# A graph network's softmax over edges: the restart penalties of the running maximum move from ScalarE to GpSimd

## What is computed

```
msg     = relu(h[src] + e) + 1e-7            e = edge_attr @ We + be
m       = msg * t
seg_max = segment_max(m, dst)
ex      = exp(m - seg_max[dst])
agg     = segment_sum(msg * ex, dst) / segment_sum(ex, dst)
z       = relu(layernorm((h + agg) @ w1 + b1)) @ w2 + b2
```

## Time and profile before

| | |
|---|---|
| median of 3 runs | 3566.0 us (3565.28 to 3567.18) |
| profiled execution, span from first to last instruction | 4412.7 us |
| mean granted TensorE clock in it | 0.771 |
| POOL busy | 2517.9 us (57%), 2621 instructions |
| PE busy | 2914.6 us (66%) |
| DVE busy | 2824.3 us (64%) |
| ACT busy | 1741.2 us (39%) |

### The profile page before, as it was taken

One profiled execution on the slowest core, in us unless ns is written; L12 is line 12 of the kernel. 1 busy time (PEld: TensorE's weight loads), 2 busy tenths in 40 slices (PEclk: granted clock), 3 DMA queues, 4 the chain that ended last, 5 costly groups with the idle time before them and its releaser, 6 DMA issues.

```text
span 4412.7 us, 44760 instructions
## 1 busy us (share of the span) xinstructions
PE 2914.6 (66%) x16648; PEld 1382.9 (31%) x16648; DVE 2824.3 (64%) x2795; ACT 1741.2 (39%) x2192; POOL 2517.9 (57%) x2621
## 2 busy tenths in 40 slices
PE   3667677775437776777435777777742777777764
PEld 2223233332313333333222333333331333333333
DVE  6467678778436665666753666665763565666675
ACT  3356555545223333333432333333432333433343
POOL 6565656564366665666445666665627565655642
PEclk6778788877568888888656888887855787888875
DMA  6677778877237777777534777777734677777761
GB/s 153 162 219 204 215 195 222 219 198 174 59 100 204 204 204 192 204 204 204 133 81 115 204 204 204 205 205 201 191 76 104 160 199 199 204 202 190 211 153 40
DMA packets 1041338, 774.25 MB, mean 175 GB/s; under 512 B 914394, under 2 KB 935391, under 8 KB 1017504
## 3 DMA queue, kind: packets, MB, share of 16 engines
q1 hardware_dynamic: 934256, 446.17, 42.9%
q10 hardware_dynamic: 22048, 226.63, 14.0%
q0 software_dynamic: 84816, 98.59, 9.9%
HBM read 478.68 MB, written 292.44 MB: 175 GB/s over the span
## 4 chain that ended last, share of the span: by engine, by line
PE 41%; issue 23%; DVE 11%; ACT 10%; another core or an unknown queue 10%; POOL 4%; DMA 1%; SPq 0%; ACTq 0%; POOLq 0%; DVEq 0%
PE X L537 32%; PE X L520 5%; POOL gath L479 4%; DVE decay L885 3%; PE X L547 2%; DVE state_all L916 2%; ACT msg L647 2%; DVE X L890 1%; ACT shared L676 1%; ACT X L649 1%; ACT decay L659 1%; ACT X L664 1%; DVE state_all L900 1%; ACT decay L637 1%
## 5 line engine op out<-in xcount | busy, mean ns | idle before, releaser
L479 POOL DMA_INDIRECT gath<-z_table,idx x2488 | 2396.0, 963 | 1606.0 <-issue 750.5
L537 PE MATMUL X<-one_hot,z_parts 128*64 128x512 fp8e5 x13800 | 2103.0, 427 | 840.8 <-issue 773.1
L537 PEld LDWEIGHTS X<-one_hot,z_parts 128*64 128x64 bf16 x13800 | 939.4, 120 | 2071.2 <-issue 1542.8
L883 DVE TENSOR_TENSOR decay<-decay,top 128x1 f32<-128x1 f32 x216 | 34.2, 158 | 1358.5 <-ACT X L649 1179.6
L647 ACT ACTIVATE msg<-X,edge_bias 128x1024 f32<-128x1024 f32 (+2 forms) x216 | 228.2, 1057 | 1622.5 <-remote 1080.3
L520 PE MATMUL X<-attr,enc_edge 128*128 128x512 f32 x824 | 469.3, 688 | 221.9 <-issue 115.8
L659 ACT ACTIVATE decay<-X 128x1024 f32<-128x1024 f32 (+2 forms) x216 | 209.3, 969 | 791.7 <-DVE X L890 556.1
L871 DVE STREAM_TRANSPOSE rows_all<-state_all 128x1024 f32<-128x1024 f32 (+3 forms) x432 | 505.9, 1171 | 7.5
L885 DVE TENSOR_TENSOR_SCAN decay<-X,decay 128x1023 f32<-128x1023 f32 (+2 forms) x216 | 477.2, 2209 | 7.7
L900 DVE TENSOR_TENSOR_SCAN state_all<-decay,state_all,X 128x1024 f32<-128x1024 f32 (+2 forms) x216 | 468.2, 2167 | 20.0 <-ACT X L664 16.0
L916 DVE TENSOR_TENSOR_SCAN state_all<-decay,state_all,X 128x1024 f32<-128x1024 f32 (+2 forms) x216 | 468.0, 2167 | 0.0
(11 more groups left out here) (155 smaller groups left out, 1182.3 us busy)
## 6 DMA issues: line engine op xcount, KB each, us to landing
rows_table<-rows_all SPq DMA_DIRECT2D x784, 256.0 KB
one_hot<-one_hot_dram ACTq DMA_DIRECT2D x69, 1920.0 KB
attr<-attr_t SPq DMA_DIRECT2D x196, 512.0 KB
one_hot<-one_hot_dram ACTq DMA_DIRECT2D x69, 1280.0 KB
one_hot_dram<-one_hot SPq DMA_DIRECT2D x23, 1920.0 KB
gath<-z_table,idx POOLq DMA_INDIRECT x2488
one_hot_dram<-one_hot SPq DMA_DIRECT2D x23, 1280.0 KB
keep<-keep_dram SPq DMA_DIRECT2D x192, 128.0 KB
```

Of the source, the lines that this page charges most:

```text
L479: pool.indirect_dma_start(out=gath[s][:, n * F:(n + 1) * F], out_offset=None, in_=z_table, in_offset=bass.IndirectOffsetOnAxis(ap=idx[:, c ...
L537: last = nc.tensor.matmul(x[h * F:(h + 1) * F, BANK:CH], z_parts[:, i * GB + k, third, :], one_hot[:, i, k, h * BANK:(h + 1) * BANK], star ...
```

## The change

The function `penalties` moves from ACT's stream to POOL's, as a `tensor_scalar` with a multiply and an add. POOL makes the penalties of chunk c - 2 while it is at the gathers of chunk c: ahead of the ninth where the chunk has 16, and ahead of the first where it has fewer. The last two of a layer follow its last gathers. The waits for `keep_landed` and `num_ready` move along.

```diff
--- before.py
+++ after.py
@@ -46,6 +46,7 @@
 KEY_SLOTS = 3
 KEEP_CHUNKS = 2
 KEEP_SLOTS = 2
+LEAD = 2
 NKEEP = -(-NCH // KEEP_CHUNKS)
 GB = 5
 PIECES_1H = NT // GB
@@ -462,6 +463,17 @@
                                         in_offset=bass.IndirectOffsetOnAxis(ap=row_i[:, i:i + 1], axis=0))\
                     .then_inc(keys_gathered[i % KEY_SLOTS], 16)
 
+            def penalties(layer, c):
+                g = layer * NCH + c
+                s = g % SLOTS
+                w = width(c)
+                k, at = layer * NKEEP + c // KEEP_CHUNKS, STARTS[c] - STARTS[c - c % KEEP_CHUNKS]
+                pool.wait_ge(keep_landed[k % KEEP_SLOTS], 16 * HALVES * (k // KEEP_SLOTS + 1))
+                if g >= SLOTS:
+                    pool.wait_ge(num_ready, g - SLOTS + 1)
+                nc.gpsimd.tensor_scalar(decay[s][:, 0:w], keep8[k % KEEP_SLOTS][:, at:at + w], BIG, -BIG, ALU.mult, ALU.add)\
+                    .then_inc(pen_ready, 1)
+
             for layer in range(LAYERS):
                 if layer == 0:
                     pool.wait_ge(idx_landed, 16)
@@ -474,7 +486,10 @@
                     if g >= SLOTS:
                         pool.wait_ge(x_ready, g - SLOTS + 1)
                     settle()
+                    pause = KT if gathered_tiles(layer, c) == KT else first_tile(c) * HALVES
                     for n in range(first_tile(c) * HALVES, gathered_tiles(layer, c) * HALVES):
+                        if n == pause and c >= LEAD:
+                            penalties(layer, c - LEAD)
                         col = STARTS[c] // P * HALVES + n
                         pool.indirect_dma_start(out=gath[s][:, n * F:(n + 1) * F], out_offset=None, in_=z_table,
                                                 in_offset=bass.IndirectOffsetOnAxis(ap=idx[:, col:col + 1], axis=0))\
@@ -482,6 +497,8 @@
                     if layer == 0 and c in PREP_CHUNKS:
                         gather_keys(c - PREP_CHUNKS[0])
 
+                for c in range(NCH - LEAD, NCH):
+                    penalties(layer, c)
                 pool.wait_ge(stored[0], 16 * NSTORE * ((layer + 1) * NCH // 2 + ((layer + 1) * NCH) % 2))
                 pool.wait_ge(stored[1], 16 * NSTORE * ((layer + 1) * NCH // 2))
                 pool.wait_ge(ends_stored, 16 * (layer + 1))
@@ -626,17 +643,6 @@
 
         @block.scalar
         def _(act):
-            def penalties(layer, c):
-                g = layer * NCH + c
-                s = g % SLOTS
-                w = width(c)
-                k, at = layer * NKEEP + c // KEEP_CHUNKS, STARTS[c] - STARTS[c - c % KEEP_CHUNKS]
-                act.wait_ge(keep_landed[k % KEEP_SLOTS], 16 * HALVES * (k // KEEP_SLOTS + 1))
-                if g >= SLOTS:
-                    act.wait_ge(num_ready, g - SLOTS + 1)
-                nc.scalar.activation(decay[s][:, 0:w], keep8[k % KEEP_SLOTS][:, at:at + w], ACT.Copy,
-                                     scale=BIG, bias=-BIG).then_inc(pen_ready, 1)
-
             def messages(layer, c):
                 g = layer * NCH + c
                 s = g % SLOTS
@@ -742,10 +748,8 @@
             act.wait_ge(consts_set, 5)
             for layer in range(LAYERS):
                 for c in range(NCH):
-                    if c == 0:
-                        penalties(layer, 0)
-                        if layer == 0:
-                            act.wait_ge(t_landed, 16)
+                    if layer == 0 and c == 0:
+                        act.wait_ge(t_landed, 16)
                     messages(layer, c)
                     n = one_hot_bank(layer, c + 3)
                     building = n is not None and built_in(layer, n)
@@ -754,8 +758,6 @@
                     exponents(layer, c)
                     if building:
                         spread_lanes(n, range(2, GB))
-                    if c < NCH - 1:
-                        penalties(layer, c + 1)
                     if layer == 0 and c in PREP_CHUNKS:
                         count_keys(c - PREP_CHUNKS[0])
                     if layer > 0:
```

## The result

| | before | after |
|---|---|---|
| median | 3565.64 us (4 runs, 3564.68 to 3567.18) | 3776.74 us (4 runs, 3773.53 to 3778.55) |
| ratio, 95% interval | | 1.0591 (1.0577 to 1.0604) |
| profiled execution, span | 4412.7 us | 3773.6 us |

The change makes the kernel 211 us slower; forecast were 279. One thing must be said of the profiles: that of the kernel before shown above is of an execution like those of a second chip, on which the same kernel takes 4423 us (median of 7); the timed runs are like those of a first chip, on which it takes 3567. The span of the kernel after is within 3 us of its median.

A forecast was written before the change was run, and what follows sets the result against it. POOL's gathers were taken to bound the timed execution. 3566 us plus 252 (280 us of penalties on POOL, a tenth hidden) plus 27 at the layers' ends gave 3845 us, range 3555 to 3950.

The forecast's parts named there:

- The bound: POOL's gathers bound the timed execution, 30 us for a pair of chunks, with hardly any wait for PE.
- partly hidden: POOL bounds only part of each layer, PE or transfers the rest; half is hidden: 3706 us or less, chance 0.08.
- wholly hidden: The 0.30 us between gathers are the profiler's, so POOL's slack takes in the 280 us: 3566, chance 0.09.
- faster: POOL has slack and DVE waits for ACT, so `m` comes up to 0.97 us earlier: 3514 us, chance 0.14.
- profiled execution's frame: In the longer profiled execution penalties fit into POOL's waits for PE, so its span grows less, to 4440 to 4520 us.
- The instructions: 216 penalties on POOL: 225 us for the columns at 1.09 ns each, plus 23 us fixed at 0.105 each.
- The step to the neighbours: Step between a gather and a penalty on POOL, 0 to 0.30 us: 0.15 taken, 32 us in all.
- A tenth hidden: A tenth of POOL's added 280 us is covered, in nearly tied layer 0 and the fill of the layers, leaving +252.
- The layers' ends: At each layer's end the last full chunk's penalties come later and DVE starts 6.8 us later: 4 × 6.8 = +27 us.
- The sign named for it: A longer wait of POOL ahead of L494 was to show the cost at the layers' ends; no size given.
- POOL and DVE hold each other up: Penalties beside DVE's building of banks in layer 0 wait as gathers do: 76 us more, 3921, chance 0.06.
- The moved waits: Mid-layer, later penalties hold nothing up: the way to `x_ready` takes about 20 us, POOL needs it some 40 us later.

The follow-up runs named there:

- runs 1 to 3: run 1, run 2, and the kernel before with 78 gathers left out in layers 1 to 3: 3470.7 us.
- ACT twice: The kernel before with ACT making the penalties twice, the first time into a tile that nobody reads: 3567.2 us, ratio 0.9999.
- run 1: The kernel before, unchanged, for a second profile: 3565.3 us.
- run 2: The kernel before with ACT's penalties kept and POOL making as many on tiles of its own (the copies): 3762.4 us, ratio 1.0553.

## Why the prediction was right

**The bound.** Right, and by the argument given: POOL's own stream, added up, left no room in 3566 us for the waits for PE that the profile showed. The rivals *partly hidden* and *wholly hidden* are out (runs 1 to 3), *faster* too (ACT twice: 0.9999). One reason in it was wrong: the 846.7 us between span and median are not of profiling, as run 1 has a span of 3563.3 us for a time of 3565.3. By PE's single matmuls, which only the second chip's profiles share, they are most likely of that chip. With this the sentence on the "profiled execution's frame" falls. The span was forecast at 4440 to 4520 and is 3773.6, simply the kernel's time on the chip of the timed runs. The argument held since POOL's own durations are the same in both (963 and 967 ns a gather, 0.30 a step). The waits for others that it took from that frame were 144 us too long and the end 15 us. That is where the 114 us came from by which its sum exceeded the median; of the two explanations that it gave, the shorter ends of the layers were the right one.

**The sum.** 279 forecast, 211 measured, term by term:
- The instructions: 248 us (225 + 23) forecast, 217 measured. The slope is 0.86 ns, near the memset's 0.78 and not in the middle with 1.40; the fixed part is 0.19 us, not 0.105.
- The step to the neighbours: +32 us forecast, between 0 and 65. Measured is less than nothing: 0.99 us from gather to gather for an instruction of 1.06, about -15 us in all. The bound was wrong on this side: a tensor instruction after a gather saves a part of the gather's 0.30, and "below nothing" was left out without a reason. This is the largest error, 47 us.
- A tenth hidden, -28 us: some 10 were, and not where it was put. Even the nearly tied layer 0 has no cover between its gathers: the copies of run 2 make it 52.6 us longer from first to last gather (7 of these us are the held-up copies), layer 1 49.8. What is covered lies behind the last gathers, where the ends of the four layers are 9 to 10 us shorter than in run 1.
- Together these are 252 us forecast; the rows give 217 - 15 - 10 = 192, and run 2 gave 195, with 7 us of held-up copies in layer 0.
- The layers' ends: 27 us forecast. The changed kernel is 14 us over the copies, 21 without the 7 us that those were held up, and one chunk less of lead gives 14 back. The mechanism fits: later penalties, later end. The sign named for it did not come, a longer wait ahead of the gathers of the sums: POOL waits 52.7 us for the stores there (28.5 + 24.2) and waited 99.5 in run 1. The cost came earlier, as the waits at the last penalties.

By the cycles of the Trainium skill (GPSIMD Engine Reference, section 3.1) the columns would cost an estimated 178 us at 1.03 cycles a column; the measured slope gives 177. The rows agree with that figure and not with the 1.8 cycles.

**The lock.** The rival *POOL and DVE hold each other up* was right in kind and small in time: 7 us in the copies of run 2, under 1 us in the changed kernel, where 76 were feared. DVE's and POOL's timeline, once in the changed kernel:

```profile
574.44 1.09 DVE L890 SCALAR_TENSOR_TENSOR top<-msg,tcol,decay 128x1 f32<-128x1 f32 x1
574.45 1.06 POOL L474 TENSOR_SCALAR decay<-keep 128x1024 f32<-128x1024 uint8 x1
```

L890 has two inputs in SBUF and takes 1.09 us instead of 0.22, as long as the penalties beside it. By the rule of the Trainium skill (SBUF — State Buffer, "Who interferes with whom") the two contend, and the trace agrees. It happened once to L890 in 216 (its mean grew from 221 to 229 ns), and DVE has time. Beside the building of a bank (L981) one of the changed kernel's penalties was held up, to 1.46 us. In run 2 it was 17 copies; each began 0.92 us after an L996, which had 0.56 us to go, and took 0.4 us longer than it does alone, and DVE's next instruction was held up in its turn: L996 2.32 us instead of 1.48, or the one-column L900 0.99 instead of 0.16.

**The moved waits.** Right in the middle of the layers at `LEAD = 2`. That the same loop decides at 3 was within reach: the prediction gave 20 against 40 us, measured are 24.4 against 43, and the third chunk of lead takes 21 off the 43.

## What to carry to other kernels

Add up the stream of each engine with its steps between instructions, and hold the sum against the timed median before believing the busy shares: POOL at 71% was the bound beside DVE at 79%, as the steps between its gathers count as idle. A microsecond there was about one in the result, while 213 us more on ACT (49%) cost nothing. A span far from the median may be of another chip; take a second profile on the one that is timed before explaining the difference. When work moves to an engine that runs ahead, draw the loop back to it: against one chunk behind, two cost 14 us and three 325, as the way round the loop then took 24.4 us and POOL's stream left 22.2.

## What the runs showed of the hardware

- A POOL gather of 128 rows takes 0.94 us and a step of 0.30 to the next gather, but a tensor instruction starts within 0.03 us of its end, and the gather behind it after 0.17. Between gathers, a tensor instruction of 1.06 us costs 0.99.
- POOL makes bytes into float32 with a multiply and an add at 0.86 ns a column plus 0.19 us; ACT needs 1.04 us for the same 1024 columns.
- The same program takes 3567 us on one chip and 4423 on another. POOL's gathers and DVE's scans last the same. In the profiles of the slower one PE has stretches in which it issues one matmul in more than a microsecond and waits for nothing that is shown.
- A byte-to-float32 instruction on POOL that starts while DVE is at an int32 `tensor_tensor` of 128x1280 (1.48 us) doesn't finish its 1.06 us beside it: 17 of 17 that began 0.92 us after one took 1.46 us or more.
- PE's edge product of four matmuls takes 1.88 us at a granted clock of 1.00 and 3.75 at 0.50, which it had behind 9.76 us of idling.
